# Attention on one core: the turned row maxima move ahead of the value burst, both rows go out from ScalarE inside it, and the eighth score moves ahead of the turns of the output

## The reference, cut to what matters

```python
x = x + layernorm(attention(layernorm(x), w_qkv))        # x: 4 x 2048 x 512
x = x + layernorm(mixed_ffn(layernorm(x), gates, W, TW)) # 8 experts' weights mixed per batch row
# attention: 16 heads of 32, windows of 128 queries; a window sees the keys of
# the window before it, its own and the one after it (fewer at the two ends)
scores = einsum('bhnqe,bhnke->bhnqk', q * scale, k_ctx)
attn   = softmax(where(valid, scores, -1e9))
out    = einsum('bhnqk,bhnke->bhnqe', attn, v_ctx)
```

## Time and profile before

| | |
|---|---|
| median of three executions | 2940.21 us |
| profiled execution, its own time | 2937.19 us |
| its span in the profile | 2935.3 us |
| busy: TensorE, VectorE, ScalarE, GpSimd | 98%, 68%, 59%, 29% of the span |
| first and last turn of maxima (L649) | 553.2 and 1265.8 us |
| last turn of the output (L688) | 1290.7 us |

### The profile page before, as it was taken

How to read it: one execution, slowest core, us unless ns; L and a number is a source line. 1 busy time by engine, 2 the same in 40 slices (tenths; PEclk the granted TensorE clock), 3 DMA queues, 4 the chain that set the end, 5 groups by cost and what they waited for, 6 DMA issues and landing times.

```text
span 2935.3 us, 55438 instructions
## 1 busy us (share of the span) xinstructions
PE 2867.0 (98%) x20252; PEld 2378.8 (81%) x20252; DVE 1994.9 (68%) x3769; ACT 1727.5 (59%) x3385; POOL 853.4 (29%) x713
## 2 busy tenths in 40 slices
PE   8999999999999999989989999999999999999998
PEld 6888888788888887778767888788888888888886
DVE  5333333488888887888868766886768766796664
ACT  3222222377767776665636666866667666676666
POOL 1000000188888887974400000500005000040003
PEclk9999999999999999999989999999999999999999
DMA  6555555678788889959999866985769765895642
GB/s 215 184 174 171 183 186 194 221 191 199 196 198 199 198 201 216 227 180 399 389 394 333 286 208 207 354 319 200 254 212 404 265 205 199 289 399 196 232 137 86
DMA packets 361429, 697.10 MB, mean 237 GB/s; under 512 B 26576, under 2 KB 127056, under 8 KB 361184
## 3 DMA queue, kind: packets, MB, share of 16 engines
q1 hardware_dynamic: 335456, 629.63, 67.0%
q10 hardware_dynamic: 17424, 32.24, 3.1%
q0 software_dynamic: 8304, 31.98, 2.7%
HBM read 525.45 MB, written 167.78 MB: 236 GB/s over the span
## 4 chain that ended last, share of the span: by engine, by line
PE 83%; DMA 6%; DVE 4%; issue 3%; ACT 2%; POOL 2%; ACTq 0%; DVEq 0%; SPq 0%; POOLq 0%
PE a_acc L571 18%; PE e_acc L1407 7%; PE e_hid L1390 7%; PE e_hid L1391 7%; PE e_hid L1392 7%; PE e_acc L1409 7%; PE e_acc L1408 7%; PE a_ps_score L622 5%; PE a_ps_keys L641 5%; PE a_ps_out L670 5%; DMA a_q_st<-a_max_rows 3%; DMA a_gate_att<-o_scratch 3%; PE a_ps_out L678 2%; PE a_ps_turn L688 1%; POOL a_gate_x L1231 1%
## 5 line engine op out<-in xcount | busy, mean ns | idle before, releaser
L1780 DVE SCALAR_TENSOR_TENSOR e_part<-e_ring,e_g_cols,e_part 128x512 f32<-128x512 f32 x896 | 647.5, 778 | 5.7 <-DMA e_ring<-mix_rows 3.2
L487 DVE TENSOR_REDUCE a_neg_max<-a_ps_score 128x1 f32<-128x384 f32 (+1 forms) x1024 | 490.1, 526 | 48.8 <-PE a_ps_score L622 47.5
L323 POOL TENSOR_TENSOR a_total<-a_probs 128x512 f32<-128x512 f32 x256 | 323.8, 1281 | 591.5 <-ACT a_probs L415 591.2
L415 ACT ACTIVATE a_probs<-a_ps_keys 128x384 f32<-128x384 f32 (+1 forms) x1024 | 422.8, 477 | 46.3 <-PE a_ps_keys L641 22.8
L1804 DVE TENSOR_TENSOR e_u_lo<-e_u,e_u_hi 128x512 fp32r<-128x512 f32 x256 | 180.0, 703 | 372.8 <-ACT e_u_hi L1538 372.6
L1534 ACT ACTIVATE e_u<-e_hid,e_mb 128x512 f32<-128x512 f32 x256 | 176.9, 691 | 432.0 <-PE e_hid L1392 419.4
L1263 POOL TENSOR_SCALAR e_var<-e_moments 128x4 f32<-128x4 f32 x15 | 6.7, 445 | 1273.4 <-DVE e_moments L1816 1272.7
L622 PE MATMUL a_ps_score<-a_k_st,a_q_st 96*128 96x384 f32 (+1 forms) x1024 | 332.5, 359 | 3.7 <-DMA a_q_st<-qk_scratch 2.8
L641 PE MATMUL a_ps_keys<-a_q_st,a_k_st 97*128 97x384 f32 (+1 forms) x1024 | 318.8, 353 | 12.3 <-DMA a_q_st<-a_max_rows 11.2
L333 POOL TENSOR_TENSOR a_total<-a_total,a_probs 128x512 f32<-128x512 f32 x224 | 286.3, 1281 | 58.0 <-ACT a_probs L415 55.5
L467 DVE TENSOR_TENSOR a_qk<-a_acc,a_qk 128x512 fp32r<-128x512 f32 x128 | 88.1, 690 | 308.1 <-ACT a_qk L364 308.1
(11 more groups left out here) (154 smaller groups left out, 6465.8 us busy)
## 6 DMA issues: line engine op xcount, KB each, us to landing
e_ring<-mix_rows SPq DMA_DIRECT2D x558, 512.0 KB, 5.5
qk_scratch<-a_qk SPq DMA_DIRECT2D x128, 512.0 KB, 3.3
a_k_st<-qk_scratch SPq DMA_DIRECT2D x180, 256.0 KB, 4.4
a_q_st<-qk_scratch SPq DMA_DIRECT2D x180, 256.0 KB, 4.4
v_scratch<-a_v SPq DMA_DIRECT2D x64, 256.0 KB, 3.1
a_v_sb<-v_scratch SPq DMA_DIRECT2D x64, 256.0 KB, 5.0
o_scratch<-a_out SPq DMA_DIRECT2D x128, 128.0 KB, 3.1
x_scratch<-a_gate_x POOLq DMA_DIRECT2D x16, 1024.0 KB, 10.2
```

Source lines behind the costliest of these rows:

```text
L323: add = pool.tensor_tensor(total[:, g % 2, i], p[0], p[1], ALU.add)
L415: act.activation(probs[:, m % PROBS, h, 0:(hi - lo) * WIN], ps_keys[x % TRIO][:, 0:(hi - lo) * WIN], ACT.Exp, scale=SCALE).then_inc(exp_do ...
L487: dve.tensor_reduce(neg_max[:, g % 2, i, h:h + 1], ps_score[y % TRIO][:, 0:(hi - lo) * WIN], AX_X, ALU.max, negate=True).then_inc(reduced, 1)
L1780: dve.scalar_tensor_tensor(out=part[:, n % 2, half, :], in0=ring[:, slot, :], scalar=g_cols[:, b, e:e + 1], in1=so_far, op0=ALU.mult, op1= ...
```

## The change

turn_max of group T+2 comes right after s2, ahead of the burst. For all but the first two groups it writes to the ps_keys bank that k0 of group T has just used (and k3 will use), so it waits for the exponential of k0 in place of a normalisation, and k3 waits for rows_done (the copy of the rows). On VectorE copy_rows comes after reduction 0 in place of reduction 2. Both rows are sent from ScalarE's queue, after the exponential of k2 and ahead of copy_out; SP sends none in the steps. On TensorE s7 comes before turn_out and k7 in place of after them. turn_out no longer waits for rows_done. Splitting `normalise` into `invert` and `normalise` changes no order.

```diff
@@ -189,6 +189,12 @@
         def load_k(eng, n, c):
             load_stack(eng, n, c, k_st, 1, (0, 0, 1), k_loaded)
 
+        def turned_max(g):
+
+            if g < AHEAD - 1:
+                return ps_turn[0:2 * QH, 0, :]
+            return ps_keys[UNITS * (g - AHEAD + 1) % TRIO][0:2 * QH, 0:WIN]
+
         def send_row(eng, g, i):
             w = 2 * (g % HALF) + i
             eng.wait_ge(rows_done, g + 1)
@@ -275,8 +281,6 @@
                 if T >= 5 and T % 2 == 1 and n + 1 < ROUNDS:
                     sp.wait_ge(pv_done, T - 2)
                     load_v(n + 1, c)
-                if there(T + AHEAD - 1):
-                    send_row(sp, T + AHEAD - 1, 1)
                 if T == 0:
                     sp.wait_ge(v_done, TILES * (CHUNKS + 1))
                     for p in range(2):
@@ -426,13 +430,14 @@
                 for x in range(3):
                     if there(T):
                         weights(T, x)
+                if there(T + AHEAD - 1):
+                    for i in range(2):
+                        send_row(act, T + AHEAD - 1, i)
                 if there(T - LAG):
                     copy_out(T - LAG)
                 for x in range(3, UNITS):
                     if there(T):
                         weights(T, x)
-                    if x == 4 and there(T + AHEAD - 1):
-                        send_row(act, T + AHEAD - 1, 0)
                 along(T)
 
         def vector(dve, along):
@@ -492,11 +497,13 @@
                     for i in range(2):
                         dve.wait_ge(rows_landed[i][g % 2], 16 * (g // 2))
                 dve.wait_ge(max_turned, g + 1)
-                dve.tensor_copy(max_rows[:, g % 2, :], ps_turn[0:2 * QH, 0, :]).then_inc(rows_done, 1)
-
-            def normalise(g):
+                dve.tensor_copy(max_rows[:, g % 2, :], turned_max(g)).then_inc(rows_done, 1)
+
+            def invert(g):
                 dve.wait_ge(out_turned, g + 1)
                 dve.reciprocal(inv_sum[:, g % 2], ps_turn[:, 3, :].rearrange("p (h e) -> p e h", e=E)[:, 0:2, :]).then_inc(inv_done, 1)
+
+            def normalise(g):
                 dve.wait_ge(inv_done, g + 1)
                 if g >= 2:
                     dve.wait_ge(out_stored[g % 2], 16 * (g // 2))
@@ -543,14 +550,14 @@
                     copy_rows(1)
             for T in range(STEPS + LAG):
                 if there(T + AHEAD):
-                    for s in range(3):
-                        reduce(T + AHEAD, s)
+                    reduce(T + AHEAD, 0)
                 if there(T + AHEAD - 1):
                     copy_rows(T + AHEAD - 1)
                 if there(T + AHEAD):
-                    for s in range(3, UNITS):
+                    for s in range(1, UNITS):
                         reduce(T + AHEAD, s)
                 if there(T - LAG):
+                    invert(T - LAG)
                     normalise(T - LAG)
                 along(T)
 
@@ -633,6 +640,8 @@
                     pe.wait_ge(rows_landed[1][g % 2], 16 * (g // 2 + 1))
                 if x == QH and g % HALF != HALF - 1:
                     pe.wait_ge(rows_landed[0][(g + 1) % 2], 16 * ((g + 1) // 2 + 1))
+                if x == TRIO and there(g + AHEAD - 1):
+                    pe.wait_ge(rows_done, g + AHEAD)
                 x += 8 * g
                 if x >= TRIO:
                     pe.wait_ge(exp_done, x - TRIO + 1)
@@ -643,10 +652,9 @@
 
             def turn_max(g):
                 pe.wait_ge(reduced, UNITS * (g + 1))
-                turned = g - AHEAD - LAG + 1
-                if turned > 0:
-                    pe.wait_ge(norm_done, turned)
-                pe.transpose(ps_turn[0:2 * QH, 0, :], neg_max[:, g % 2].rearrange("p w h -> p (w h)"), ident[:, :])\
+                if g >= AHEAD - 1:
+                    pe.wait_ge(exp_done, UNITS * (g - AHEAD + 1) + 1)
+                pe.transpose(turned_max(g), neg_max[:, g % 2].rearrange("p w h -> p (w h)"), ident[:, :])\
                   .then_inc(max_turned, 1)
 
             def values(g):
@@ -681,7 +689,6 @@
 
             def turn_out(g):
                 pe.wait_ge(out_copied, g + 1)
-                pe.wait_ge(rows_done, min(g + LAG + AHEAD, STEPS))
                 if g >= 1:
                     pe.wait_ge(norm_done, g)
                 for i in range(3):
@@ -736,22 +743,22 @@
                 scores(T, [1])
                 all_keys(T, [1, 2])
                 scores(T, [2])
+                if there(T + AHEAD - 1):
+                    turn_max(T + AHEAD - 1)
                 if there(T - LAG):
                     values(T - LAG)
                     sums(T - LAG)
                 along(T)
-                if there(T + AHEAD - 1):
-                    turn_max(T + AHEAD - 1)
                 scores(T, [3])
                 all_keys(T, [3])
                 scores(T, [4])
                 all_keys(T, [4, 5])
                 scores(T, [5, 6])
                 all_keys(T, [6])
+                scores(T, [7])
                 if there(T - LAG):
                     turn_out(T - LAG)
                 all_keys(T, [7])
-                scores(T, [7])
 
         ends = dict(reduced=reduced, norm_done=norm_done, exp_done=exp_done, out_copied=out_copied, out_stored=out_stored)
         return (sync, gpsimd, scalar, vector, tensor), gate_front, ends
```

## The result

The changed kernel takes 2957.78 us (median of 8 executions) against 2937.99 us for the kernel before on the same chip (8 executions): ratio 1.0082, 95% interval 1.007 to 1.0094. That is 20 us slower. The forecast was 2944 us, range 2915 to 2966, with the kernel before at 2940.21. The difference is over the 14.7 us that count here, so this is the outcome "slower", to which the prediction gave 0.26.

The account below looks back on a forecast made before the run. TensorE's own work plus its gaps was taken to bound the step. Terms +15 (94 steps), +1 and +2 (later steps), -14 (rows) sum to +4 on the profiled 2937.2 us, 3.0 under the median: 2944 us, range 2915 to 2966.

Parts of the forecast that it names:

- Rival C: Row sends: rows stay late because the DMA engines are the limit; 2958 us, chance 0.11.
- VectorE in the burst: Reduction 3 starts earlier, so the gap at s6 falls from 0.14 to 0.03: -0.11 us a full step.
- s7 ahead of the output's turns: On TensorE, s7 must wait for reduction 4 to free its bank: +0.12 us a full step.
- k7 loses its cover: One matmul less between k7 and the next step's k2, which waits for exponential 7: +0.15 us a full step.
- The turn ahead of the burst: On TensorE, the turn between s2 and the burst delays the burst's start: +0.08 us a full step.
- The turn leaves the place after the burst: On TensorE, k3 starts no sooner, since s3's uncovered weight load takes the turn's time: 0.0 saved.
- Both rows on ScalarE: In the burst, both issues stay hidden ahead of copy_out, with 0.2 to 0.4 us in hand.
- turning point of 4.73: On ScalarE, rows_done later than 4.73 us makes copy_out late; each 0.1 beyond costs 0.1 of a step.
- +0.16 a step: Average over full and short steps: new gaps 0.25 and 0.08, less some 0.17 of old ones; +15 us over 94 steps.
- rows' -14: Key waits for landed rows: earlier sends win back 14 of 16 us, clock loss included; bounds 0 and -18.
- Rival A: On TensorE, the gaps at s7 and k2 don't open: -6 us for the stage, 2918 us, chance 0.23.
- Rival D: The change does nothing that counts, gaps only change place: 2940 us, chance 0.05.

Follow-up runs that it names:

- three_issues: s7_back_k0_first with row 1 sent in two halves, so that three issues stand ahead of copy_out: 2993.46 us, ratio 1.0199 to the kernel before.
- sends_back: The changed kernel with rows sent as before (row 1 by SP, row 0 by ScalarE behind k4's exponential): 2959.48 us, ratio 1.009 to the kernel before.
- s7_back_k0_first: The changed kernel with s7 put back behind the output's turns and k7, and k0 ahead of s0: 2930.66 us, ratio 0.9996 to the kernel before.
- s7_back_k0_first_sends_back: s7_back_k0_first with rows sent as before (row 1 by SP, row 0 by ScalarE behind k4's exponential): 2942.87 us, ratio 1.0032 to the kernel before.

## Why the prediction was right, and where it was off

2957.78 us lies in the range, but the size was off: +20 where +4 was forecast. It lies just outside the 2930 to 2957 that the prediction gave its own sum; it is inside 2915 to 2966 only because that range takes in the rivals too. Rival C's 2958 fits by chance, for C had the rows stay late, and they don't. What held is the mechanism of a full step. By the prediction's own steps:

- *VectorE in the burst*, -0.11: measured -0.11 (k6 0.38 after the pair s5, s6, from 0.49). Right.
- *s7 ahead of the output's turns*, +0.12: measured, from k6 to the transposes 0.47 where two free distances are 0.35. Right.
- *k7 loses its cover*, +0.15: from the pair k1, k2 (905.01) to s2 (905.50) it is 0.49 in place of 0.35, so 0.14. Right.
- *The turn ahead of the burst*, +0.08: measured +0.13 (0.43 from s2 to the burst, from 0.30). 0.05 of it is the wait for exponential 0, which I had called met with 0.05 in hand. I had given the turn the distances of a held weight load (0.05); it starts 0.15 after the exponential's end. The other 0.08 is the turn's place, as forecast.
- *The turn leaves the place after the burst*, 0.0: right, 0.28 from s3 to k3 against 0.29.
- *Both rows on ScalarE*: hidden, as forecast; three_issues shows how near the edge. The prediction's turning point of 4.73 is a slip: 1.02 before the burst's end at 5.61 is 4.59. rows_done came at 4.28 (906.41), so there was 0.3 in hand.

Together +0.24 was forecast for a full step, and +0.26 measured (5.42 to 5.68). The first step that failed is the one from the full step to the average, "+0.16 a step": it let the gaps go in the steps with short windows and took too much off for the old ones. In the trace those steps lose as well: in the cycle of eight, five steps lose 0.26 to 0.27 and three lose 0.14 to 0.18, where the prediction's terms left these three 0.09 to 0.12. At 910 us, where the scores are short, the cover of k7 shrinks with them, and k2 waits even longer:

```profile
910.72 0.19 PEld L650 LDWEIGHTS a_ps_keys<-a_q_st,a_k_st 97*128 97x128 f32 x1 [0.25 <-ACT a_probs L419]
```

The changed kernel is 0.2 us behind at the end of the second burst and 18.5 at the burst of group 96, with the 3.4 us of old row waits won back on the way. That is 0.23 a step, and some 6 us more than the +15 that were forecast.

The second, and the larger miss, lies in the last 31 steps. There +3 was forecast for gaps and ScalarE, and most of the rows' -14, together some 8 us won. Nothing was won: the last burst ends 18.5 us later as well.

```profile
1288.43 0.47 PE L1317 MATMUL e_bank<-e_yt,e_cw_hi 128*128 128x512 f32 x1 [1.42 <-DVE e_yt L1692]
...
1306.96 0.47 PE L1324 MATMUL e_bank<-e_yt,e_cw_hi 128*128 128x512 f32 x1 [1.42 <-DVE e_yt L1699]
```

Both are the first matmul after the last burst, the first line in the kernel before and the second in the changed one. The waits for rows did go, 3.4 and 10.8 us, but not their worth. In their place stand the gaps of the step, which the prediction counted at a quarter here (0.23 in each of 31 steps would be 7 us, an estimate), and new waits of the turn: for reductions 6.0 us, from 1.8, and for exponentials 3.3 us, from none. The prediction had the further pieces of VectorE in these steps delay ScalarE, but not the turn, which now holds the whole burst. How the miss divides among these isn't shown.

Loads of queries took the rows' place only in part. The weights of the scores wait 5.0 us for them, but they waited 3.8 before. In the chain of waits from 1150 to 1320 us they hold 12.3%, where before, from 1150 to 1300, rows held 13.5%. So rival C's mechanism, loads met instead of rows, is real but small here. By sends_back the earlier send itself is worth about 2 us in this kernel, and in s7_back_k0_first 12.

Rival A (whose -0.09 a step would make -8 up to 1100 us and not -6) fell: of the 90 steps to 1100 us, the scores were held by a reduction in 89, and the keys by an exponential 80 times. Rival D is excluded by the interval.

## What to carry to other kernels

Before one item of an in-order queue is moved, count what stood between each producer and its consumer: s7 covered exponential 7 and itself needed reduction 4, and it cost 14 us to move it, where removing a visible gap of 0.14 gave 0.11 a step. A buffer that is reused earlier hands its new user the wait for its last reader, and the profile may book that wait as "issue"; the distance from the reader's end shows it. And write the ledger for the short steps too: the average of a cycle isn't the full step less the terms that look smaller.

## What the runs showed that I had not expected

A matmul that waits for two semaphores in turn starts 0.14 to 0.15 us after the later one's producer ends, in the changed kernel, in s7_back and, for k0, in s7_back_k0_first_sends_back. The weights of one with a single wait start 0.05 after it (0.16 for its effect on the next). That the second wait makes this difference isn't shown. A turn of 8 columns ahead of the burst costs 0.09 to 0.12 there; the same turn behind the burst cost nothing that could be read. The Trainium skill (TensorEngine Tiling (Array Packing), Key Properties) says that a change of tiling mode drains TensorE; the measured 0.21 from the turn to the burst, for a matmul of 0.27, agrees with that, and the number of such changes in a step is the same on both sides. But counting the changes alone would have made the turn's new place free, and it wasn't.
